# First attention stage of a two-layer transformer block: maxima rounded on GpSimd, merged products, 64-column masks, a split run of value matmuls, and another order on SyncE's queue

## The chip, the cores and the metric

One core of one Trainium2 chip. The metric is the device time of one execution in microseconds (us), the median of the runs shown. One execution was also taken by the hardware profiler; all rows below come from it.

The names of the profile: PE is TensorE's matmul stream and PEld its weight loads, DVE is VectorE, ACT is ScalarE, POOL is GpSimd, SP is SyncE, which here does nothing but issue DMAs.

## What is computed

Two pre-norm layers on x of 4 x 1024 tokens with 128 features. Only the first stage of the first layer is touched by the change, causal attention with 16 heads of 8 features and a bias that depends on the distance of query and key:

```python
q, k, v = (x @ W.T + b) split into 16 heads of 8
sim  = einsum('bhid,bhjd->bhij', q, k) + bias[i, j] * SCALE     # bias: 32 distance buckets
sim  = sim + causal                                             # -inf where j > i
out  = softmax(sim) @ v ;  out @ Wo.T + bo
```

Behind it come a routed feed-forward layer (16 leaves), a wide attention over its outputs, a second attention stage without a mask in this form, and a gated feed-forward layer. Those stages stay as they are.

## The kernel before

The stage is `attend_causal` (from line 508). It works through 64 heads (`NG`, 16 heads of 4 batches), one after the other, and in a pass of the loop, which this document calls head n's **pass**, the engines work on several heads at once. q and k are each split into three bf16 parts, so that a product of full precision is six bf16 products, stacked along the contraction: 48 rows (`PROWS`). Because 48 rows fit in half of the array, every operand is loaded twice, into partitions 0 to 47 and 64 to 111, and matmuls alternate between the two halves ("row groups"), which run side by side.

For each head:

- **Maxima** (lines 700 to 723). PE writes the masked scores of a query block against all keys into `psM` (two buffers of 1024 columns). There are five units, `MAXIMA = [(7,), (0, 6), (1, 5), (2, 4), (3,)]`, each of one or two query blocks. The mask is added by two further matmuls of 128 columns (`mask`, lines 694 to 698), whose operands lie in `masks`. DVE takes the row maxima with 8 reductions of 128 to 1024 columns (line 615), and then rounds minus the maximum to bf16 in two instructions, the value and the rest (lines 625 and 627). A unit waits until DVE has taken the unit two before it. The first unit of a head also waits for that head's loads (line 709).
- **Shift rows**. PE turns the rounded maxima with one small matmul (`rows`, line 733), ACT copies them to SBUF (line 666), and SP issues two small DMAs that put them under the head's q operand (`load_r`, line 505), where they act as two more contraction rows (50 in all).
- **Scores** (lines 736 to 752). Nine units of 512 columns into a ring of three banks (`psS`); a unit waits until ACT has taken the unit three before it. Those that touch the diagonal get the mask, again two matmuls of 128 columns. ACT takes the exponential (line 686) into `probs`. Unit 0 waits for the shift rows' DMA (line 739).
- **Bias near the diagonal**. POOL multiplies 8 blocks of `probs` (7 of 256 columns, one of 128) by the table of exponentiated biases (line 654). It also stages the values of the next head (line 645).
- **Values** (lines 754 to 776). 26 fp32 products in three parts, written to four column groups of the array (32 columns each), which run side by side; a product is two instructions for each of 10 wide (256 columns) and 16 narrow (128 columns) ones. Part 0 has 13 products, parts 1 and 2 six and seven. ACT copies the result (line 672), SP stores it (`store_o`, line 494).

The order on PE is written out by hand (lines 783 to 801): in head n's pass it does the scores of head n, the maxima of head n + 2 and the values of head n - 1:

```python
scores(n,0) scores(n,1) maxima(n+2,0) maxima(n+2,1) scores(n,2) scores(n,3)
values(n-1,0) rows(n+1) scores(n,4) maxima(n+2,2) scores(n,5) scores(n,6) maxima(n+2,3)
values(n-1,1) scores(n,7) scores(n,8) maxima(n+2,4) values(n-1,2)
```

SP's order is also by hand (lines 584 to 590). The loads of a head (`load_s`) are four DMAs of 96 KB; q and k have six buffers each (`BUFS`):

```python
for n in range(NG):
    load_s(n + 4)      # q and k of head n+4; waits for scores of head n-2
    store_o(n - 2)     # waits for ACT's copy of head n-2, in pass n
    load_r(n + 1)      # waits for ACT's copy of the shift rows, in pass n
```

So SP's round n ends in the middle of pass n, where `rows(n+1)` stands, and round n + 1 begins at once with the loads of head n + 5.

The opening stage `project_heads` builds the masks on POOL (lines 308 to 315, three selections), and SP swaps their halves with two DMAs (line 217).

## Time and profile before

| | us |
|---|---|
| median of 3 runs | 1780.42 (1780.28 to 1783.19) |
| profiled execution, its own time | 1783.86 |
| span of its trace, first to last instruction | 1782.1 |
| stage in question, from its first to its last matmul | 65.5 to 498.3 |
| share of the span: PE, DVE, ACT, POOL | 91%, 85%, 72%, 46% |
| granted TensorE clock, mean over the span | 0.943 |

The span is the time from the first to the last instruction; what lies between it and the execution's time (1.8 us) is outside the program. The share of an engine is the sum of its instructions' times, and those of overlapping matmuls are counted once, so that a PE at 91% may still have room in it. The granted clock is 1.00 at 2.4 GHz and 0.50 at 1.2 GHz. In the rows below, a line such as `L747 MATMUL heads_psS<-one_qS,one_kS 50*128 50x512 bf16 x2` is a group of instructions of line 747 that write tile `psS` from `qS` and `kS`, 50 rows of 128 stationary columns against 512 moving columns.

### The profile page before, as it was taken

The numbers are of one execution on the slowest core, as the hardware profiler recorded it, in microseconds if no ns is written. First come the engines' busy times: TensorE is split into PE (matmuls) and PEld (weight loads), VectorE is DVE, ScalarE is ACT, GpSimd is POOL, SyncE is SP. The second block draws the span as 40 slices with busy tenths as digits, with TensorE's granted clock in tenths as the row PEclk, the third lists the DMA queues.
The fourth block names the chain that finished last, engine by engine and source line by source line (L and its number), as shares of the span: only waits on it lengthen the run. The fifth ranks groups of instructions, "written<-read, shape, count | busy, mean of one in ns | idle before, by whom it ended". The sixth has DMA issues, their size and how long they took to land. (4 is left out here: it accounts for less than half of the span.)

```text
span 1782.1 us, 47495 instructions
## 1 busy us (share of the span) xinstructions
PE 1613.3 (91%) x18834; PEld 1038.2 (58%) x18858; DVE 1518.7 (85%) x2248; ACT 1276.2 (72%) x2523; POOL 817.8 (46%) x1533
## 2 busy tenths in 40 slices
PE   5599999999976999999899549999999999999966
PEld 3376667666665887877688314444444444444544
DVE  8699999999856999988677768999999999999735
ACT  6488878888834444454565628888989898998955
POOL 5488888888845001000340323444444444444446
PEclk9699999999965999999999868999999999999978
DMA  7522222323172766565000351111121121112031
GB/s 247 207 85 86 87 90 87 98 86 98 52 148 45 97 95 91 93 90 69 0 1 1 144 184 47 56 56 55 59 65 59 52 73 51 60 53 71 26 76 48
DMA packets 119910, 141.89 MB, mean 80 GB/s; under 512 B 22221, under 2 KB 80778, under 8 KB 119690
## 3 DMA queue, kind: packets, MB, share of 16 engines
q1 hardware_dynamic: 119258, 138.79, 30.8%
q8 instruction: 150, 2.46, 0.6%
q14 instruction: 70, 0.57, 0.1%
q10 hardware_dynamic: 432, 0.07, 0.0%
HBM read 92.70 MB, written 44.98 MB: 77 GB/s over the span
## 5 line engine op out<-in xcount | busy, mean ns | idle before, releaser
L888 DVE TENSOR_REDUCE heads_mx<-heads_psM 128x1 f32<-128x1024 f32 x512 | 602.1, 1219 | 48.4 <-PE heads_psM L979 32.2
L959 ACT ACTIVATE heads_probs<-heads_psS 128x512 f32<-128x512 f32 x1024 | 546.1, 601 | 77.7 <-PE heads_psS L1002 71.7
L928 POOL TENSOR_TENSOR heads_masked<-heads_probs,g_tri 128x128 f32<-128x128 f32 x512 | 233.7, 456 | 360.8 <-ACT heads_probs L959 360.7
L654 POOL TENSOR_TENSOR heads_probs<-heads_probs,one_ebias 128x256 f32<-128x256 f32 (+1 forms) x512 | 341.6, 689 | 76.8 <-ACT heads_probs L686 76.1
L615 DVE TENSOR_REDUCE heads_mx<-heads_psM 128x1 f32<-128x1024 f32 (+7 forms) x512 | 348.8, 748 | 23.7 <-PE heads_psM L697 23.0
L686 ACT ACTIVATE heads_probs<-heads_psS 128x512 f32<-128x512 f32 x576 | 316.3, 603 | 67.6 <-PE heads_psS L697 62.4
L979 PE MATMUL heads_psM<-three_kS,three_qS 48*128 48x512 bf16 x1024 | 230.4, 395 | 20.5 <-PEq L2050 11.6
L1002 PE MATMUL heads_psS<-three_qS,three_kS 50*128 50x512 bf16 x1024 | 238.0, 389 | 0.7 <-ACT heads_probs L959 0.3
L1510 ACT ACTIVATE trees_hid_hi<-trees_hid 128x512 fp32r<-128x512 f32 x192 | 121.6, 633 | 152.4 <-DVE trees_hid L1531 151.5
L1531 DVE SCALAR_TENSOR_TENSOR trees_hid<-trees_psH,g_b,trees_chosen 128x512 f32<-128x512 f32 x192 | 143.8, 749 | 31.8 <-DMA trees_chosen<-leaf_choice 15.1
L1027 PE MATMUL heads_psO<-heads_probs,heads_ones_only 128*32 128x128 f32 x1920 | 162.0, 284 | 0.0
L719 PE MATMUL heads_psM<-one_kS,one_qS 48*128 48x512 bf16 (+3 forms) x768 | 147.5, 334 | 14.8 <-PEq L2050 11.6
L1028 PE MATMUL heads_psO<-heads_probs,heads_v_ones 128*32 128x128 f32 x1920 | 155.9, 273 | 0.0
L769 PE MATMUL heads_psO<-heads_probs,heads_v_ones 128*32 128x256 f32 x1280 | 150.3, 394 | 2.2 <-POOL heads_probs L654 2.0
L747 PE MATMUL heads_psS<-one_qS,one_kS 50*128 50x512 bf16 (+3 forms) x768 | 141.1, 332 | 11.2 <-DMA one_qS<-heads_mrow 9.5
L1021 PE MATMUL heads_psO<-heads_probs,heads_ones_only 128*32 128x256 f32 x1280 | 148.7, 390 | 0.0
L1002 PEld LDWEIGHTS heads_psS<-three_qS,three_kS 50*128 50x128 bf16 x1024 | 69.5, 93 | 114.6 <-ACT heads_probs L959 55.3
L773 PE MATMUL heads_psO<-heads_probs,heads_v_ones 128*32 128x128 f32 x2048 | 136.1, 279 | 0.0
L1538 DVE SCALAR_TENSOR_TENSOR trees_hid_lo<-trees_hid,trees_hid_hi 128x512 fp32r<-128x512 f32 x192 | 134.0, 698 | 0.1
L1021 PE MATMUL heads_psO<-heads_probs,heads_v_ones 128*32 128x256 f32 x768 | 121.3, 394 | 0.0
L1027 PEld LDWEIGHTS heads_psO<-heads_probs,heads_ones_only 128*32 128x32 f32 x1920 | 72.6, 108 | 82.7 <-issue 82.7
L979 PEld LDWEIGHTS heads_psM<-three_kS,three_qS 48*128 48x128 bf16 x1024 | 56.4, 94 | 96.2 <-DVE heads_mx L888 64.5
(273 smaller groups left out, 3174.3 us busy)
## 6 DMA issues: line engine op xcount, KB each, us to landing
trees_chosen<-leaf_choice SPq DMA_DIRECT2D x96, 256.0 KB, 7.6
head_outputs<-g_small SPq DMA_DIRECT2D x128, 128.0 KB
one_qS<-q_parts SPq DMA_DIRECT2D x128, 96.0 KB
one_kS<-k_parts SPq DMA_DIRECT2D x128, 96.0 KB
three_qS<-q_parts SPq DMA_DIRECT2D x128, 96.0 KB
three_kS<-k_parts SPq DMA_DIRECT2D x128, 96.0 KB
q_parts<-g_w SPq DMA_DIRECT2D x8, 768.0 KB, 4.6
k_parts<-g_w SPq DMA_DIRECT2D x8, 768.0 KB, 5.8
```

What stands on the lines that cost most here:

```text
L615: last = dve.tensor_reduce(mx[:, p, qb:qb + 1], psM[(n * NM + i) % 2][:, at:at + w], AXX, ALU.max)
L654: pool.tensor_tensor(pr[:, a:a + w], pr[:, a:a + w], bass.AP(eb.tensor, eb.offset + NEAR - 1, [list(eb.ap[0]), [-1, w]]), ALU.mult).then_i ...
L686: act.activation(probs[n % 2][:, slot * CH:(slot + 1) * CH], ring.bank(i)[:, :], ACT.Exp).then_inc(slot_taken, 1)
L769: last = pe.matmul(out.rearrange("p (q w) -> p q w", w=P), v[:, kb, :], bass.AP(pr.tensor, a, [list(pr.ap[0]), [far - a, 2], [1, P]]), sta ...
L888: dve.tensor_reduce(mx[:, n % 2, k:k + 1], psM[k % 2][:, :], AXX, ALU.max, negate=True).then_inc(max_taken, 1)
L928: pool.tensor_tensor(masked[n % 2][:, kb, :], probs[n % 2][:, kb, kb * P:(kb + 1) * P], g["tri"][:, 0:P], ALU.mult).then_inc(near_done, 1)
L959: act.activation(probs[n % 2][:, kb, h * CH:(h + 1) * CH], ring.bank(i)[:, :], ACT.Exp).then_inc(slot_taken, 1)
L979: last = pe.matmul(psM[k % 2][:, h * CH:(h + 1) * CH], qS[u][r:r + PROWS, k * P:(k + 1) * P], kS[u][r:r + PROWS, h * CH:(h + 1) * CH], sta ...
L1002: pe.matmul(ring.bank(i)[:, :], kS[u][r:r + RROWS, kb * P:(kb + 1) * P], qS[u][r:r + RROWS, h * CH:(h + 1) * CH], start=True, stop=True).t ...
L1021: pe.matmul(out.rearrange("p (q w) -> p q w", w=P), v_ones[v][:, kb, :] if kb < c else ones_only[:, :], both, start=kb == 0, stop=False, t ...
L1027: pe.matmul(out[:, 0:P], ones_only[:, :], pr[:, c, :], start=False, stop=False, tile_position=(0, c * VW))
L1028: pe.matmul(out[:, P:2 * P], v_ones[v][:, kb, :], pr[:, b, :], start=False, stop=False, tile_position=(0, c * VW))
```

## The change

What it does, part by part:

1. **Rounding on POOL.** DVE's reductions give minus the maximum (`negate=True`). The two rounding instructions leave DVE; POOL does both (`minus_maxima`), for head n + 2 in pass n, between the last two of its bias products. For heads 0 and 1 it does them ahead of its loop.
2. **Merged products.** POOL's 8 bias products become 5 instructions: blocks 0 and 1 together, 7, 6, 2 and 3 together, 5 and 4 together (up to 512 columns).
3. **Masks of 64 columns.** A mask is still two matmuls with 128 stationary columns, but each covers 64 moving columns and not 128. Within a unit of the maxima the products of both row groups come first, in turn, and the masks at the end. The opening builds two tables with 14 small selections on POOL, each of which waits for the one before; SP copies with one DMA.
4. **Split value run.** Four parts of 6, 3, 10 and 7 products; part 1 stands right behind `rows`. Part 0 waits for four of the five bias products, part 2 for all.
5. **Maxima further ahead on PE.** The first two units are done for head n + 3, in the second half of pass n, and units 2, 3, 4 for head n + 2.
6. **Order on SP.** In each round the shift rows of head n + 1 come first, then the store of head n - 2, then the loads of head n + 4.

```diff
@@ SP's rounds
             for n in range(NG):
+                if n + 1 < NG:
+                    load_r(n + 1)
+                if n >= 2:
+                    store_o(n - 2)
                 if n + 4 < NG:
                     load_s(n + 4)
-                if n >= 2:
-                    store_o(n - 2)
-                if n + 1 < NG:
-                    load_r(n + 1)
@@ DVE
-                        last = dve.tensor_reduce(mx[...], psM[...][:, at:at + w], AXX, ALU.max)
+                        last = dve.tensor_reduce(mx[...], psM[...][:, at:at + w], AXX, ALU.max, negate=True)
...
-                dve.tensor_scalar(nm[:, p, 0, :], mx[:, p, :], -1.0, None, ALU.mult).then_inc(nm_hi, 1)
-                dve.wait_ge(nm_hi, n + 1)
-                dve.scalar_tensor_tensor(nm[:, p, 1, :], mx[:, p, :], -1.0, nm[:, p, 0, :], ALU.mult, ALU.subtract).then_inc(nm_ready, 1)
@@ POOL
+    NEARS = [((0, 1), 2), ((7,), 3), ((6,), 5), ((2, 3), 6), ((5, 4), 8)]
+            def minus_maxima(n):
+                p = n % 2
+                pool.wait_ge(max_taken, (n + 1) * NM)
...
+                pool.tensor_copy(nm[:, p, 0, :], mx[:, p, :]).then_inc(nm_hi, 1)
+                pool.wait_ge(nm_hi, n + 1)
+                pool.tensor_tensor(nm[:, p, 1, :], mx[:, p, :], nm[:, p, 0, :], ALU.subtract).then_inc(nm_ready, 1)
...
+                for blocks, unit in NEARS:
                     pool.wait_ge(slot_taken, ring.index(n, unit) + 1)
+                    weight(n, blocks)
+                    if unit == NEARS[-2][1] and n + 2 < NG:
+                        minus_maxima(n + 2)
@@ PE: masks, values
+                m2 = g["masks"][r:r + HALF, table, :]
+                for half in range(2):
+                    done = pe.matmul(out[:, half * HALF:(half + 1) * HALF], m2[:, half * P:(half + 1) * P], m2[:, 2 * P:2 * P + HALF],
+                                     start=False, stop=stop and half == 1)
...
-                    pe.wait_ge(near_done, (n + 1) * TPB)
+                    pe.wait_ge(near_done, n * len(NEARS) + NEAR_FIRST)
...
+                if part == 2:
+                    pe.wait_ge(near_done, (n + 1) * len(NEARS))
+    VALUES = [[(0, 0), (1, 0), (2, 0), (3, 0), (0, 1), (1, 1)], [(2, 1), (3, 1), (0, 2)],
+              [(1, 2), (2, 2), (3, 2), (0, 3), (1, 3), (2, 3), (3, 4), (0, 4), (1, 4), (0, 5)],
+              [(2, 4), (3, 3), (0, 6), (1, 5), (2, 5), (0, 7), (1, 6)]]
@@ PE's order
+            maxima(2, 0)
+            maxima(2, 1)
             for n in range(NG):
                 scores(n, 0)
                 scores(n, 1)
-                maxima(n + 2, 0)
-                maxima(n + 2, 1)
+                maxima(n + 2, 2)
+                maxima(n + 2, 3)
                 scores(n, 2)
                 scores(n, 3)
                 values(n - 1, 0)
                 rows(n + 1)
+                values(n - 1, 1)
                 scores(n, 4)
-                maxima(n + 2, 2)
+                maxima(n + 2, 4)
                 scores(n, 5)
                 scores(n, 6)
-                maxima(n + 2, 3)
-                values(n - 1, 1)
+                maxima(n + 3, 0)
+                values(n - 1, 2)
                 scores(n, 7)
                 scores(n, 8)
-                maxima(n + 2, 4)
-                values(n - 1, 2)
+                maxima(n + 3, 1)
+                values(n - 1, 3)
```

## Rows read from the trace of the kernel before

**Rows 1.** Busy time by stretch: the stage's settled part (engine busy us, granted clock, DMA share).

```profile
96.60:475.00 378.40, 368.56 (x6348) 261.05 (x6346) 363.68 (x583) 312.87 (x641) 319.55 (x525) 1.00 0.29 88
```

**Rows 2.** One line's instructions: ACT's copies of the shift rows, one for each head.

```profile
L666 ACT ACTIVATE heads_mrow<-heads_psS x64: 249/267/267, 72.6 to 484.2; 16x128 bf16<-16x128 f32 x64
```

**Rows 3.** Timeline of PE, one pass of a head (start us, us, instructions).

```profile
279.91 0.40 PE L747 MATMUL heads_psS<-one_qS,one_kS 50*128 50x512 bf16 x2
...
281.53 0.64 PE L769 MATMUL heads_psO<-heads_probs,heads_v_ones 128*32 128x256 f32 x8
...
282.64 0.22 PE L733 MATMUL heads_psS<-g_identb,heads_nm 128*16 128x128 bf16 x1
282.79 0.39 PE L747 MATMUL heads_psS<-one_qS,one_kS 50*128 50x512 bf16 x1
283.02 0.27 PE L697 MATMUL heads_psS<-g_masks 64*128 64x128 bf16 x2
283.13 0.39 PE L719 MATMUL heads_psM<-one_kS,one_qS 48*128 48x256 bf16 x2
...
284.27 0.30 PE L773 MATMUL heads_psO<-heads_probs,heads_v_ones 128*32 128x128 f32 x2
...
284.84 0.40 PE L747 MATMUL heads_psS<-one_qS,one_kS 50*128 50x128 bf16 x3
...
285.62 0.31 PE L773 MATMUL heads_psO<-heads_probs,heads_v_ones 128*32 128x128 f32 x3
...
286.19 0.40 PE L747 MATMUL heads_psS<-one_qS,one_kS 50*128 50x512 bf16 x2
```

**Rows 4.** Timeline of ACT in the same pass: the exponential of unit 0.

```profile
280.44 0.60 ACT L686 ACTIVATE heads_probs<-heads_psS 128x512 f32<-128x512 f32 x1 [0.26 <-PE heads_psS L697]
```

**Rows 5.** DVE: the reductions of one head (timeline), and the first rounding instruction (all 64).

```profile
281.35 5.42 DVE L615 TENSOR_REDUCE heads_mx<-heads_psM 128x1 f32<-128x1024 f32 x8
...
L625 DVE TENSOR_SCALAR heads_nm<-heads_mx x64: 171/704/710, 71.8 to 481.8; 128x8 bf16<-128x8 f32 x64
```

**Rows 6.** POOL: its products of 256 columns (96.6 to 475 us); the later stage's rounding.

```profile
L654 POOL TENSOR_TENSOR heads_probs<-heads_probs,one_ebias 128x256 f32<-128x256 f32 x409 | 287.8, 723 | 58.8 <-ACT heads_probs L686 58.4
...
L911 POOL TENSOR_TENSOR heads_nm<-heads_mx,heads_nm x64: 199/200/202, 1053.4 to 1685.9; 128x8 bf16<-128x8 f32 x64
```

**Rows 7.** Timeline of POOL in the opening stage (the wait stands in brackets).

```profile
16.80 1.27 POOL L327 TENSOR_TENSOR g_x<-g_x,g_bo 128x512 f32<-128x512 f32 x1 [7.52 <-DMA g_bo<-in_L_attn_bo]
```

**Rows 8.** Timeline of SP's queue, one round (start us, us of issuing).

```profile
283.19 1.38 SPq L505 DMA_DIRECT2D one_qS<-heads_mrow  x2
284.61 1.54 SPq L490 DMA_DIRECT2D one_qS<-q_parts  x2
286.20 1.41 SPq L490 DMA_DIRECT2D one_kS<-k_parts  x2
287.65 0.58 SPq L494 DMA_DIRECT2D head_outputs<-g_small  x1
```

**Rows 9.** SP's last load of head 5; DMA traffic from 83 to 91 us in 40 slices; one DMA's landing.

```profile
84.61 1.41 SPq L490 DMA_DIRECT2D one_kS<-k_parts  x2
...
GB/s 0 0 0 21 0 0 0 31 72 41 82 164 123 82 72 133 164 123 102 164 123 51 113 133 133 41 20 0 0 0 0 0 0 9 12 0 82 21 0 0
...
g_x<-in_L_attn_x SPq DMA_DIRECT2D x8, 256.0 KB, 3.9
```

**Rows 10.** Waits, 96.6 to 475 us (total us, times, longest): scores for the shift rows' DMA.

```profile
PEld heads_psS L747 <- DMA one_qS<-heads_mrow: 17.3, 30, 1.7
```

**Rows 11.** PE around the one fall of the clock in the stage (timeline; busy time by stretch).

```profile
234.12 0.40 PE L747 MATMUL heads_psS<-one_qS,one_kS 50*128 50x512 bf16 x2 [1.44 <-DMA one_qS<-heads_mrow]
...
235.30:238.70 3.40, 3.40 (x35) 2.06 (x34) 2.11 (x3) 1.86 (x5) 1.86 (x3) 0.50 0.22 69
...
241.96 0.40 PE L747 MATMUL heads_psS<-one_qS,one_kS 50*128 50x512 bf16 x2
```

**Rows 12.** Timeline of PE at the stage's start: the shift rows of head 1.

```profile
80.21 0.28 PE L733 MATMUL heads_psS<-g_identb,heads_nm 128*16 128x128 bf16 x1
```

More of the change, by code:

```diff
@@ L60 @@
 SHIFTS = 2
+MASKW = 2 * P + HALF
 EARLY = 2
@@ L693, in _, with mask @@
         def _(pe):
-            def mask(out, r, table):
-                for s in range(2):
-                    done = pe.matmul(out, g["masks"][r:r + HALF, s, 0, :], g["masks"][r:r + HALF, s, table, :], start=False, stop=s == 1)
+            def mask(out, r, table, stop=True):
+                m2 = g["masks"][r:r + HALF, table, :]
+                for half in range(2):
+                    done = pe.matmul(out[:, half * HALF:(half + 1) * HALF], m2[:, half * P:(half + 1) * P], m2[:, 2 * P:2 * P + HALF],
+                                     start=False, stop=stop and half == 1)
                 return done
@@ L710, in maxima @@
                 ps = psM[k % 2]
-                at = 0
+                runs, ends, at = ([], []), [], 0
                 for qb in MAXIMA[i]:
@@ L715, in maxima @@
                         a, z = max(at, bank * CH), min(at + w, (bank + 1) * CH)
-                        if a >= z:
-                            continue
-                        r, ends = HALF * bank, z == at + w
-                        last = pe.matmul(ps[:, a:z], qS[u][r:r + PROWS, qb * P:(qb + 1) * P], kS[u][r:r + PROWS, a - at:z - at], start=True, stop=not ends)
-                        if ends:
-                            last = mask(ps[:, z - P:z], r, 1)
-                    at += w
+                        if a < z:
+                            runs[bank].append((qb, a, z, a - at))
+                    at += w
+                    ends.append(at)
+                for j in range(max(len(of) for of in runs)):
+                    for bank in range(2):
+                        if j < len(runs[bank]):
+                            qb, a, z, first = runs[bank][j]
+                            r = HALF * bank
+                            pe.matmul(ps[:, a:z], qS[u][r:r + PROWS, qb * P:(qb + 1) * P], kS[u][r:r + PROWS, first:first + z - a],
+                                      start=j == 0, stop=j + 1 == len(runs[bank]) and (bank + 1) * CH not in [-(-e // CH) * CH for e in ends])
+                for half in range(2):
+                    for z in ends:
+                        r, at = HALF * ((z - 1) // CH), z - P + half * HALF
+                        m2, later = g["masks"][r:r + HALF, 0, :], [e for e in ends if z < e <= -(-z // CH) * CH]
+                        last = pe.matmul(ps[:, at:at + HALF], m2[:, half * P:(half + 1) * P], m2[:, 2 * P:2 * P + HALF], start=False,
+                                         stop=half == 1 and not later)
                 last.then_inc(maxima_done, 1)
@@ L749, in scores @@
                     if diagonal:
-                        last = mask(ps[:, at:at + P], r, 2)
+                        last = mask(ps[:, at:at + P], r, 1)
                     at += count
@@ L804, in _ @@
             values(NG - 1, 2)
+            values(NG - 1, 3)
 def attend_full(nc, m, g, hand, gather):
```

72 lines of the change are left out of this document (44 added, 28 removed).

## The prediction

> **What bounds the kernel now.** I read the busy time by stretch first. In the settled part of the stage PE and DVE are both nearly always busy, ACT and POOL are not [rows 1]. Two engines at the limit need a closer look, so next comes the length of a pass: the copies of the shift rows give 411.6 us for 63 passes, 6.53 us each [rows 2], while the pass in PE's timeline takes 6.28 (279.91 to 286.19) [rows 3]. The difference, 0.25 us a pass or some 15 us, is stalls, and the list of waits names one: scores that wait for the shift rows' DMA, 17.3 us in 30 times [rows 10].
>
> Who sets 6.28? DVE's 8 reductions take 5.42 [rows 5]. The first rounding instruction takes 0.704 in the middle and 0.171 at best [rows 5], so some 0.53 us of it is a wait inside the instruction. (The Trainium skill, "SBUF — State Buffer", section "Who interferes with whom", says that such an instruction and one of GpSimd exclude each other from a shared port pair; by that rule the wait ends with a product on POOL, and the trace agrees in size, 0.72 for a product.) DVE's own work is therefore about 5.42 + 0.17 + 0.17 = 5.76, and it has slack. PE has none: its pass is a chain of stretches [rows 3]. From scores 0 to the values 1.62, values part 0 1.11, rows 0.15, the second row stretch 1.48, part 1 0.57, the third row stretch 0.78, part 2 0.57: 6.28. The first of these hangs on ACT as well: the exponential of unit 0 begins at 280.44 and lasts 0.60 [rows 4], and only then may unit 3 use its bank.
>
> **The change, part by part**, for a pass in which nothing is late.
>
> *DVE* drops to 5.42. As PE sets the pass, that gives nothing by itself. *POOL* is busy 319.55 us in 378.4, 5.5 a head [rows 1]; the merged products handle as many columns, so at worst they cost the same, at best three fixed parts less; the rounding adds 2 x 0.20 [rows 6]. That is 5.9 at most, below the pass that follows; POOL is covered by PE, with little to spare. If it were not, part 2 of the values would wait for the last product.
>
> *Masks.* Two masks of 128 columns lie 0.11 us apart from start to next start (283.02 to 283.13) [rows 3]. No matmul of 64 columns is in the trace. Bounds: nothing saved (the weights still have 128 columns), or half, 0.055 a pair. I take half, since the 512 columns at 282.79 hold the next start off by 0.23, four times the 0.055 of one mask [rows 3]: the time goes with columns. The rule against it is in the Trainium skill, "TensorE: Matmul & The Clock Gate", section "LDWEIGHTS": loading takes about P / 1.2 ns for P stationary columns, an estimate of 107 ns for 128. By that rule no mask would get shorter, and those of today would lie further apart than the trace has them.
>
> *PE's stretches.* First: two pairs on the chain through ACT, 1.62 - 0.11 = 1.51. Values: one narrow instruction takes about 0.11 of its column group. Part 0 has 8 such turns in the fullest group and not 10, so 1.11 - 0.22 = 0.89 to the rows. Parts 0 and 1 with the rows between them have 8 in each group, so if the rows' matmul (16 columns) leaves the other groups running, they take 1.22 to the next scores; if all drain, 0.89 + 0.15 + 0.57 = 1.61. I take 1.22: rows follow the values today at a normal distance. Part 2 has 6 turns, not 4: 0.57 + 0.22 = 0.79. Part 3: 0.57. Second row stretch: only one of five units has its work moved off, and the fuller row group then holds three units with masks and 512 columns: 3 x 0.28 + 0.21 + 0.09 = 1.14. Third: 0.78 - 0.11 = 0.67. Sum 1.51 + 1.22 + 1.14 + 0.79 + 0.67 + 0.57 = 5.90, against 6.28. The split of the values gives back part of what the masks and the even row groups win.
>
> *SP, the step that I think decides.* Today the loads of head n + 4 are issued right behind the shift rows of head n, in the middle of pass n - 1, and are needed at the start of pass n + 2: over two passes. Afterwards they come behind the shift rows of head n + 1, in the middle of pass n, one whole pass later; and PE wants them earlier, since maxima unit 0 of head n + 4 now stands in the second row stretch of pass n + 1. That is from both sides a loss, and the wait is ahead of everything on PE's queue: values part 2, units 7 and 8, all of the next pass.
>
> How long is the way from the rows' matmul to the landed loads? Matmul to SP's first issue 0.55 (282.64 to 283.19) [rows 3, 8]. The two row DMAs with the gap 1.42, the store now ahead of the loads 0.58 + 0.07, four loads 3.00 (284.61 to 287.61) [rows 8]. Landing after the last issue: nowhere does an engine wait for these loads, so I bound it. Head 5's last load is issued until 86.02, and traffic goes on until about 88.4: at least 2.4. Above: 3.9, what a DMA of 256 KB takes from its issue [rows 9]. I take 3.2, the middle. With 0.04 to wake PE: 0.55 + 1.42 + 0.65 + 3.00 + 3.2 + 0.04 = 8.86.
>
> And from that maxima unit to the next rows' matmul, on PE: the unit and the change of mode 0.37, part 2 0.79, third stretch 0.67, part 3 0.57, first stretch 1.51, part 0 0.89: 4.80. The unit in pass n + 1 waits for loads behind the rows of pass n, and these rows come 4.80 after the unit of pass n - 1. So two passes take 8.86 + 4.80 = 13.66, one takes **6.83**, not 5.90, and PE stands still for 0.93 us in each.
>
> *The shift rows* have then more time: today they are issued 3.0 us ahead of scores 0 (283.19 to 286.19) [rows 3, 8], afterwards about 3.9. Most of their 15 us go; they are inside the 6.83.
>
> *Start and end.* Rows of head 1 stand at 80.21 [rows 12]. Two more units of maxima ahead of the loop cost DVE about 1.2 each, so 82.6. The first late unit is that of pass 1: 82.6 + 8.9 = 91.5. 59 passes later, at 91.5 + 59 x 6.83 = 494.5, comes the last one that waits; two more rows follow at + 4.8 + 5.9 = 505.2, against 484.2 today [rows 2]. The stage ends **21 us** later.
>
> *Opening.* Fourteen selections, each behind the one before, cost POOL perhaps 7 us; it waits 7.52 us there today for a DMA [rows 7], so nothing; without that cover a few us. One DMA fewer on SP lies off the path too.
>
> *Clock.* A stall of 1.44 us was followed by a stretch at 0.50 (1.2 GHz), and the next pass took 241.96 - 234.12 = 7.84, or 1.56 more than 6.28 [rows 11]; it is the only one in the settled stage. With a stall near 1 us in each pass, and passes that drift into long and short ones (only the sum of two is fixed), I allow one fall in 20 heads or so: 4 us.
>
> **Sum.** 21 + 4 = 25 us on the profiled execution's own time, 1783.86 (its span is 1782.1, 1.8 less): 1809. That execution lies 3.4 above the median of the runs, so the median becomes 1780.4 + 25 = **1805**.
>
> **Rivals.**
>
> A. *The loads are in time* and nothing else is late: the pass is 5.90 plus the 0.25 of stalls that remain for the shift rows. From 82.6, 62 passes of 6.15 end at 463.9, against 484.2: 20 us less, 1760. It speaks for it that PE, DVE and POOL all get room. Against it: the way would have to shrink from 8.86 to 2 x 5.90 - 4.80 = 7.0, and without any landing it is already 5.66, so landing would have to take 1.3 us, where traffic alone goes on for 2.4 [rows 9]. Should I have misread which head is loaded in which round, this is what is left. 13 in 100.
>
> B. *The clock.* The stall in each pass lets the clock fall in every second head: 30 x 1.56 = 47 in place of 4, some 1848. For: the one fall [rows 11]. Against: thirty waits, and one fall [rows 10, 11]. 8 in 100.
>
> C. *No change.* A pass of 6.53 as now, if the way is 8.26, with a landing of 2.6, the low bound nearly. The point from which the sign turns is there. 7 in 100.
>
> D. *The masks don't shrink*, as the rule above would have it: 0.11 more in the first stretch, 0.11 in the third, 0.06 in the unit itself: 4.80 becomes 5.08, the pass 6.97, and 59 x 0.14 = 8 us are added: 1813. 15 in 100 of the chance, inside the forecast's side.
>
> E. *The change does nothing*, because PE would wait elsewhere by the same amount: only by chance; it is within C.
>
> **How the numbers follow.** The forecast as summed has 57 in 100, D 15, B 8, C 7, A 13. The bounds of the landing, 2.4 and 3.9, move a pass by -0.40 and +0.35, so -24 and +21 us: 1781 to 1826; with D and a part of B above. The range is 1776 to 1848; it leaves out A and the worst of B. A measurement of this kernel tells 0.2%, 3.6 us, from no change. Faster by more: 0.14 (A and a little of C). Same: 0.07. Slower: 0.79.
>
> **What would show it.** In the changed kernel's list of waits, PE or its weight loads wait for the loads of q or k (the matmuls of the maxima, released by "DMA one_qS<-q_parts" or "one_kS<-k_parts"), in about 60 places of 0.9 us in the mean; the wait for the shift rows' DMA is nearly gone. The copies of the shift rows lie 6.8 apart. DVE shows idle time of about 1.4 us a head that ends with PE's maxima. SP's timeline has rows, store, loads in this order, and the loads' last issue ends some 5 us behind the first row DMA. Passes of 5.9 with no such wait would prove A; a granted clock of 0.50 in many stretches of the stage would prove B. A mask pair 0.055 us apart from the next matmul proves the halving, 0.11 proves D. If the rows' matmul is followed by part 1 only after a gap of 0.1 us or more, the value groups drained, and 0.4 us are to be added to each pass's natural length, but not to the 13.66.

## The result, and the profile after

The changed kernel takes 1831.91 us (median of 4 runs, 1821.83 to 1836.86) where the kernel before, run beside it, takes 1780.35. The ratio is 1.0278, with a 95% interval of 1.0254 to 1.0303: 51.5 us slower, where 25 were forecast. The profiled execution took 1830.29, with a span of 1828.4 and a mean granted clock of 0.932.

The busy time of the same stretch as in [rows 1] comes first (us busy and instructions of PE, weight loads, DVE, ACT, POOL, then granted clock, DMA share, GB/s):

```profile
96.60:475.00 378.40, 317.89 (x5662) 213.98 (x5662) 290.41 (x415) 265.11 (x571) 280.60 (x416) 0.94 0.25 78
```

PE was busy 368.56 us of the 378.40 before and is 317.89 now; DVE fell from 363.68 to 290.41, and the clock from 1.00 to 0.94. No engine has too much work: all of them wait. How long the stage has become stands in ACT's copies of the shift rows, the line that answers to [rows 2] (durations in ns, first and last start in us):

```profile
L701 ACT ACTIVATE heads_mrow<-heads_psS x64: 248/249/267, 72.3 to 533.4; 16x128 bf16<-16x128 f32 x64
```

From 72.3 to 533.4 it is 461.1 us, against 411.6: 49.5 more. The spans differ by 46.3, so the whole loss lies in this stage, and 3 us come back elsewhere. (The medians differ by 51.5, since the profiled execution of the kernel before lies 3.5 above its median and that of the changed kernel 1.6 below.) The list of waits from 90 to 510 us names the place (us in total, times, longest):

```profile
ACT heads_probs L721 <- PE heads_psS L733: 124.7, 166, 5.4
POOL heads_probs L680 <- ACT heads_probs L721: 99.9, 97, 4.6
DVE heads_mx L637 <- PE heads_psM L768: 91.7, 88, 3.9
PE heads_psM L762 <- DMA one_kS<-k_parts: 58.4, 31, 3.6
...
PEld heads_psS L794 <- DMA one_qS<-heads_mrow: 1.4, 7, 0.2
```

ACT, POOL and DVE wait for PE, and PE for one thing, the loads of k ahead of a maxima unit: 31 times, 1.9 us in the mean. The wait for the shift rows' DMA, 17.3 us in [rows 10], is down to 1.4. Read from behind, the chain is POOL on ACT, ACT on PE, PE on the DMA; only the last of these says what to change.

SP's queue over two rounds shows how it comes about (start, us of issuing):

```profile
443.13 1.40 SPq L527 DMA_DIRECT2D one_qS<-heads_mrow  x2
444.57 0.58 SPq L516 DMA_DIRECT2D head_outputs<-g_small  x1
445.20 1.53 SPq L512 DMA_DIRECT2D one_qS<-q_parts  x2
446.76 1.41 SPq L512 DMA_DIRECT2D one_kS<-k_parts  x2
450.98 1.40 SPq L527 DMA_DIRECT2D one_qS<-heads_mrow  x2
```

and PE's timeline of the same stretch:

```profile
445.61 0.39 PE L762 MATMUL heads_psM<-one_kS,one_qS 48*128 48x512 bf16 x2 [1.83 <-DMA one_kS<-k_parts]
...
450.25 0.22 PE L780 MATMUL heads_psS<-g_identb,heads_nm 128*16 128x128 bf16 x1
```

The order is rows, store, loads, as in the diff; the last load is issued 5.0 us behind the first row DMA. The wait in brackets ends with a load of the round before. From that unit to the next rows' matmul PE needs 450.25 - 445.61 = 4.64. Passes alternate: 5.75 to 5.9 us, then 7.8 to 8.1, where nothing else comes in between. Only from 126 to 160 us are they nearly even, five passes of 6.5 to 7.0 with stalls of 0.6 to 1.0, and no fall of the clock comes there.

The second loss is the clock. One of the stalls and what follows it (PE's timeline, then busy time by stretch):

```profile
190.63 0.39 PE L762 MATMUL heads_psM<-one_kS,one_qS 48*128 48x512 bf16 x2 [2.06 <-DMA one_kS<-k_parts]
```

```profile
192.30:195.70 3.40, 3.40 (x46) 2.31 (x41) 2.12 (x5) 2.39 (x5) 1.45 (x2) 0.50 0.34 116
195.70:199.00 3.30, 3.30 (x65) 2.20 (x63) 3.09 (x5) 2.88 (x7) 2.19 (x3) 1.00 0.03 8
```

PE stood for 2.06 us, and 1.7 us later the granted clock is 0.50 (1.2 GHz) for 3.4 us: PE is busy throughout, but 46 matmuls go through where 65 do at 1.00. The kernel before has one such fall in the settled stage [rows 11], the changed one has 12, two of them 6.8 us long.

### The profile page after: what moved, and what is told of

Its sections match the earlier page's. It is cut to its first block and busy times, and to the rows that moved or that the text cites. A ratio compares the mean times of both kernels' runs of the same rounds, so it can differ in the third digit from the quotient of the medians.

```text
span 1828.4 us, 47344 instructions
## 1 busy us (share of the span) xinstructions
PE 1600.4 (88%) x18858; PEld 1014.3 (55%) x18858; DVE 1475.2 (81%) x2120; ACT 1260.1 (69%) x2523; POOL 815.4 (45%) x1480
## 5 line engine op out<-in xcount | busy, mean ns | idle before, releaser
L637 DVE TENSOR_REDUCE heads_mx<-heads_psM 128x1 f32<-128x1024 f32 (+7 forms) x512 | 357.9, 753 | 116.2 <-PE heads_psM L768 108.0
L680 POOL TENSOR_TENSOR heads_probs<-heads_probs,one_ebias 128x512 f32<-128x512 f32 (+2 forms) x320 | 313.9, 998 | 114.9 <-ACT heads_probs L721 107.4
L762 PE MATMUL heads_psM<-one_kS,one_qS 48*128 48x512 bf16 (+3 forms) x768 | 139.4, 353 | 84.8 <-DMA one_kS<-k_parts 60.2
L818 PE MATMUL heads_psO<-heads_probs,heads_v_ones 128*32 128x256 f32 x1280 | 157.6, 400 | 1.1 <-POOL heads_probs L680 1.1
L1081 PE MATMUL heads_psO<-heads_probs,heads_v_ones 128*32 128x128 f32 x1920 | 155.9, 273 | 0.0
L822 PE MATMUL heads_psO<-heads_probs,heads_v_ones 128*32 128x128 f32 x2048 | 148.4, 295 | 0.1
L794 PE MATMUL heads_psS<-one_qS,one_kS 50*128 50x512 bf16 (+3 forms) x768 | 145.6, 346 | 1.4 <-ACT heads_probs L721 1.0
L1074 PE MATMUL heads_psO<-heads_probs,heads_v_ones 128*32 128x256 f32 x768 | 121.3, 395 | 0.0
L1080 PEld LDWEIGHTS heads_psO<-heads_probs,heads_ones_only 128*32 128x32 f32 x1920 | 72.6, 108 | 82.3 <-issue 82.3
```

The costliest lines, as they stand in the source:

```text
L637: last = dve.tensor_reduce(mx[:, p, qb:qb + 1], psM[(n * NM + i) % 2][:, at:at + w], AXX, ALU.max, negate=True)
L680: pool.tensor_tensor(at, at, by, ALU.mult).then_inc(near_done, 1)
L818: last = pe.matmul(out.rearrange("p (q w) -> p q w", w=P), v[:, kb, :], bass.AP(pr.tensor, a, [list(pr.ap[0]), [far - a, 2], [1, P]]), sta ...
L1074: pe.matmul(out.rearrange("p (q w) -> p q w", w=P), v_ones[v][:, kb, :] if kb < c else ones_only[:, :], both, start=kb == 0, stop=False, t ...
L1080: pe.matmul(out[:, 0:P], ones_only[:, :], pr[:, c, :], start=False, stop=False, tile_position=(0, c * VW))
L1081: pe.matmul(out[:, P:2 * P], v_ones[v][:, kb, :], pr[:, b, :], start=False, stop=False, tile_position=(0, c * VW))
```

## Experiments

All are compared with the kernel before; its medians beside them were 1782.28 (first four), 1782.37 (next four) and 1783.3 (last three). "Stage" is the time from the first to the last copy of the shift rows, in the profile of each; "pass" is the usual distance of two passes in which nothing is late.

| kernel | us | ratio [95%] | stage | pass |
|---|---|---|---|---|
| before | 1780.4 | 1 | 411.6 | 6.28 |
| the change | 1831.9 | 1.0278 [1.0254, 1.0303] | 461.1 | 5.75 / 8.0 |
| loads first | 1775.1 | 0.9946 [0.9927, 0.9964] | 403.9 | 5.75 |
| before + new queue order | 1781.6 | 0.9993 [0.9978, 1.0008] | 408.8 | 6.28 |
| the change, filled | 1810.5 | 1.0155 [1.0137, 1.0174] | 446.5 | 6.65 / 7.1 |
| the change, store last | 1797.2 | 1.0074 [1.0048, 1.01] | 432.6 | 5.75 / 7.4 |
| one head sooner | 1760.8 | 0.9881 [0.9867, 0.9896] | 388.2 | 5.78 |
| + rounding on DVE | 1788.6 | 1.0036 [1.0022, 1.005] | 418.5 | 6.49 |
| + masks twice | 1811.4 | 1.0161 [1.0146, 1.0176] | 444.5 | 6.85 |
| + values in three parts | 1801.1 | 1.0116 [1.0095, 1.0136] | 428.0 | 6.58 |
| + masks of 128 columns | 1773.7 | 0.9940 [0.9919, 0.9961] | 404.3 | 6.15 |
| + head outputs sooner | 1749.8 | 0.9811 [0.9795, 0.9826] | 381.3 | 5.78 |
| before + order + one sooner | 1784.4 | 1.0012 [0.9998, 1.0025] | 410.0 | 6.28 |

**Is it the queue?** The first kernel undoes nothing but SP's order.

```diff
             for n in range(NG):
-                if n + 1 < NG:
-                    load_r(n + 1)
-                if n >= 2:
-                    store_o(n - 2)
                 if n + 4 < NG:
                     load_s(n + 4)
+                if n >= 2:
+                    store_o(n - 2)
+                if n + 1 < NG:
+                    load_r(n + 1)
```

> The changed kernel with one thing undone: SyncE's round is again loads of head n + 4, store, shift rows. Theory (the late head loads are the whole loss): no wait of PE for q or k is left, a pass takes the 5.8 us that the short passes of the changed kernel show, plus about 0.25 for late shift rows; the stage gets (7.26 - 6.05) x 59 = 71 us shorter than in the changed kernel, the time is about 1760, and the clock doesn't fall more than once or twice in the stage. Rival (the PE order, the split values or the work on GpSimd cost the time): the time stays above 1800.

1775.09 us, 56.8 below the changed kernel: the order costs more than the whole loss, and the rest of the change is a small gain. It is smaller than expected. Many passes are 5.75, but they average 6.34, and the waits from 90 to 500 us say why:

```profile
PEld heads_psS L794 <- DMA one_qS<-heads_mrow: 37.4, 49, 2.3
```

The shift rows are late now, 49 times. In this order they are issued behind the loads; where their two DMAs of 4 KB landed after 1.15 us at best, many took 1.5 to 2.5, and two 3.5. (All landings here are counted from the end of the last issue.) A shorter pass has made the second-latest thing the latest.

The same order in the kernel before:

```diff
+                if n + 1 < NG:
+                    load_r(n + 1)
+                if n >= 2:
+                    store_o(n - 2)
                 if n + 4 < NG:
                     load_s(n + 4)
-                if n >= 2:
-                    store_o(n - 2)
-                if n + 1 < NG:
-                    load_r(n + 1)
```

> The kernel before with SyncE's new order and nothing else of the change. Theory (the order costs only together with the maxima unit of head n + 3 in pass n): loads of head n + 4 land some 11.3 us behind the start of pass n and are needed at the start of pass n + 2, 12.6 us behind it, so PE doesn't wait for them except when they land late; the time is 1775 to 1790. Rival (the order alone is the loss): some 1830.

1781.57, no change. So it is not the order by itself: it takes the order together with something else of the change. That the something is the maxima unit that now wants its head a pass earlier is read from the trace, where PE's wait stands at that unit and nowhere else; no run undoes PE's order alone. It agrees with the prediction's "from both sides a loss".

**Is the stall all, or does the clock add to it?** The changed kernel, with useless matmuls ahead of the wait (they write to a bank that the unit itself then overwrites):

```diff
                 if i == 0:
+                    if 3 <= n:
+                        v = (n - 3) % BUFS
+                        for _ in range(4):
+                            for r, a in ((0, 0), (HALF, CH)):
+                                pe.matmul(psM[k % 2][:, a:a + CH], qS[v][r:r + PROWS, 0:P],
+                                          kS[v][r:r + PROWS, 0:CH], start=True, stop=True)
                     pe.wait_ge(s_loaded[u], (n // BUFS + 1) * 64)
```

> The changed kernel with 8 matmuls of 512 columns (two row groups, about 0.9 us) of no use ahead of PE's wait for a head's loads, written where the unit's own products go afterwards. Theory (two passes together are fixed at 13.8 us by the way through SyncE, they drift into one of 5.8 and one of 8.0, and the long stall lets the clock fall): the short pass becomes 6.65, the long one 7.15 and more even, the idle time is filled, the clock hardly falls in the stage; the mean pass is 6.9 and the time about 1831 - 59 x 0.36 = 1810, so more work makes it faster. Rival (PE's work is what counts): 0.9 x 61 = 55 us slower, 1885.

1810.52: 21.4 us faster by doing more. The busy time of its stage:

```profile
98.00:525.00 427.00, 405.91 (x7163) 271.82 (x7160) 338.80 (x482) 315.72 (x681) 333.69 (x490) 1.00 0.26 81
```

The clock is 1.00 throughout, not one fall, and the stage is 14.6 us shorter, although each head carries eight matmuls more. The loop through SyncE is as long as before: the 26 pairs of passes without a load of 512 KB (more on these below) took 13.85 us each, those of the changed kernel without a fall 13.83. So what went is the falls, and the gain is a lower bound on what the clock cost in the changed kernel.

The way itself, made shorter by the store (0.58 and a gap):

```diff
                 if n + 1 < NG:
                     load_r(n + 1)
-                if n >= 2:
-                    store_o(n - 2)
                 if n + 4 < NG:
                     load_s(n + 4)
+                if n >= 2:
+                    store_o(n - 2)
```

> The changed kernel with the round shift rows, loads, store: the loads no longer stand behind the store, so the way through SyncE is 0.65 us shorter. Theory: two passes together take 13.8 - 0.65 = 13.15, one 6.6, stalls get shorter and the clock falls less often; 20 to 35 us less than the changed kernel, 1797 to 1812. Rival (the landing of the loads doesn't follow the time of issue, since the queue is limited by something else): within 5 us of 1831.

1797.19, at the fast end of what was expected, and 34.7 us below the changed kernel. The wait for k is 35.9 us in 34 times (90 to 490 us, since the stage is shorter) and not 58.4 in 31, and the clock falls 4 times in the stage, not 12. Moving 0.65 us out of a way that closes every second pass is worth 0.33 a pass, 19 us in 59. The rest is 15; eight falls less, at the 1.6 worked out below, would be 13 of it.

**Both late things at once.** The new order as it is, but each round loads one head further ahead; there are six buffers, so there is room.

```diff
-            for n in range(EARLY, 4):
+            for n in range(EARLY, 5):
                 load_s(n)
...
-                if n + 4 < NG:
-                    load_s(n + 4)
+                if n + 5 < NG:
+                    load_s(n + 5)
```

> The changed kernel as it is, its queue order too (shift rows, store, loads), but each round of SP loads head n + 5 and not n + 4, and the opening loads one head more. Theory: both of the late things are gone, the loads because they have a whole pass more, the shift rows because nothing is issued ahead of them. With the loads in time but ahead of the shift rows, 60 passes took 6.33 each, and the undisturbed ones among them 5.75 (scores of head 2 at 94.9, of head 61 at 468.2). All of them at 5.75 to 5.80 would put head 61 at 94.9 + 59 x 5.8 = 437, 31 us sooner: 1742 to 1748, no wait of PE for a DMA in the stage and no fall of the clock in it. Rival: the passes over 5.75 came from something other than the place of the shift rows in the queue (ACT, POOL or the traffic of the loads itself): then some 1775, as with the loads first. A second rival: the loads, now ahead of their time, hold up the landing of the shift rows by traffic, since both are then in flight together more often: 1755 to 1770.

1760.76: 71 us below the changed kernel, and 1.2% faster than the kernel before, though not the 1742 to 1748 of the first theory. The time lies in the second rival's range. The usual pass is 5.78 as expected, but the mean is 6.07. No wait for q or k is left in the list from 100 to 430 us. Of the 17 us that the 59 passes take beyond 5.78, 12.6 are in three places, one of which stands in SP's queue so:

```profile
217.09 1.41 SPq L512 DMA_DIRECT2D one_kS<-k_parts  x2
218.54 0.58 SPq L1171 DMA_DIRECT2D g_qkT<-head_outputs  x1
219.21 1.38 SPq L527 DMA_DIRECT2D one_qS<-heads_mrow  x2
```

Right ahead of the shift rows goes a transfer of 512 KB, the outputs of a batch's 16 heads; the rows landed after 4.4 us, the two passes from there took 8.75 and 8.34, and the clock fell in them (the other places: 8.59 and 8.15, with a fall, and 7.69, without; all from scores to scores). That is a cause none of my theories had. Only the 4.5 us that are left, in passes of 5.8 to 6.5, may be the second rival's traffic of the loads.

From here on, three parts of the change (the rounding, the width of the masks, the split of the values) are undone one at a time in this kernel. The merged products and PE's order stay in all of them, so their worth was not measured.

**Rounding on DVE.**

```diff
+                dve.wait_ge(max_taken, (n + 1) * NM)
+                dve.wait_ge(block_taken, (n + 1) * (TPB - NM))
+                if n >= 2:
+                    dve.wait_ge(slot_done, ring.rows(n - 2) + 1)
+                dve.tensor_scalar(nm[:, p, 0, :], mx[:, p, :], 1.0, None, ALU.mult).then_inc(nm_hi, 1)
+                dve.wait_ge(nm_hi, n + 1)
+                dve.scalar_tensor_tensor(nm[:, p, 1, :], mx[:, p, :], 1.0, nm[:, p, 0, :], ALU.mult, ALU.subtract).then_inc(nm_ready, 1)
...
-            minus_maxima(0)
-            minus_maxima(1)
...
-                    if unit == NEARS[-2][1] and n + 2 < NG:
-                        minus_maxima(n + 2)
```

> The kernel with head n + 5 loaded each round, and in it the rounding of the maxima back on DVE, one part of the change undone alone. DVE's reductions take 5.42 a pass, the pass 5.75. The two roundings bring 2 x 0.17 at best, 5.76, and 0.17 + 0.70 with the wait inside the first one, 6.29. Theory (DVE becomes the bound with them, the port wait included): passes of 5.9 to 6.3, so 8 to 30 us more than with the rounding on POOL, 1752 to 1775. Rival (the prediction's view, that this part gives nothing as PE sets the pass): within 4 us of it.

1788.58, 27.8 more, inside the 8 to 30 of the theory, though the pass of 6.49 is longer than its 6.3. DVE's timeline shows a pass without a gap:

```profile
150.52 5.62 DVE L637 TENSOR_REDUCE heads_mx<-heads_psM 128x1 f32<-128x1024 f32 x8
156.18 0.17 DVE L646 TENSOR_SCALAR heads_nm<-heads_mx 128x8 bf16<-128x8 f32 x1
156.38 0.70 DVE L648 SCALAR_TENSOR_TENSOR heads_nm<-heads_mx,heads_nm 128x8 bf16<-128x8 f32 x1
```

5.62 + 0.17 + 0.70 is 6.49, the pass. The wait has moved to the second instruction, the one with two inputs, whose shortest in the kernel before is 0.166. In all 50 heads between 100 and 430 us it ends 0.02 us behind a product on POOL; in the kernel before it is the first instruction that does so, in all 51, 0.03 us behind. (By the Trainium skill, "SBUF — State Buffer", section "Who interferes with whom", a DVE instruction with two inputs in SBUF contends with a GpSimd instruction that reads there; this trace agrees, with 0.70 against 0.17.)

**Masks, first the wrong way round: each 64-column mask twice.**

```diff
                 for half in range(2):
+                    pe.matmul(out[:, half * HALF:(half + 1) * HALF], m2[:, half * P:(half + 1) * P], m2[:, 2 * P:2 * P + HALF],
+                              start=False, stop=False)
                     done = pe.matmul(out[:, half * HALF:(half + 1) * HALF], m2[:, half * P:(half + 1) * P], m2[:, 2 * P:2 * P + HALF],
```

> The kernel with head n + 5 loaded each round, with each 64-column mask matmul issued twice (the second adds the same mask again, so the output is not the reference's), which gives back about the 0.055 us per pair that the narrower masks saved. The prediction's stretches hold some 5 pairs on PE's path of a pass (two in the first, two in the third, one in the unit of maxima): 5 x 0.03 to 5 x 0.055 = 0.15 to 0.28 a pass if PE sets the pass, 9 to 17 us in all. Rival: PE has slack in the pass of 5.75 beside DVE's 5.42 and ACT, and less than 5 us are added.

1811.37, 50.6 more, three times the most that was expected. PE's timeline has the masks 0.03 us apart:

```profile
117.68 0.19 PE L733 MATMUL heads_psS<-g_masks 64*128 64x64 bf16 x1
117.71 0.19 PE L735 MATMUL heads_psS<-g_masks 64*128 64x64 bf16 x1
117.74 0.19 PE L733 MATMUL heads_psS<-g_masks 64*128 64x64 bf16 x1
117.77 0.19 PE L735 MATMUL heads_psS<-g_masks 64*128 64x64 bf16 x1
```

and the pass is 1.07 longer, which is 32 more masks at 33 ns: every added one counts in full. I then took this for the worth of the narrow masks. It isn't: issuing an operation twice is not the opposite of making it half as wide. So the width alone was undone, with zeros beside the 64 columns:

```diff
-MASKW = 2 * P + HALF
+MASKW = 2 * P + 3 * HALF
...
-                    done = pe.matmul(out[:, half * HALF:(half + 1) * HALF], m2[:, half * P:(half + 1) * P], m2[:, 2 * P:2 * P + HALF],
+                    done = pe.matmul(out, m2[:, half * P:(half + 1) * P], m2[:, 2 * P + HALF - half * HALF:3 * P + HALF - half * HALF],
```

(the same in the maxima; the table's triangle stands 64 columns further right).

> The kernel that loads head n + 5 each round, with the masks 128 columns wide again: the moving side gets 64 columns of zeros before or behind its 64, so the same values are added by as many instructions, in the same order, and only the width is undone. Doubling the 32 masks of 64 columns took 1.07 us more a pass, 33 ns each. Theory: the price of a mask goes with its columns, 55 to 60 ns at 128 and 33 at 64, so 32 x 0.022 to 0.027 = 0.7 to 0.85 a pass at most, and 0.5 at least, since the kernel before needed 6.28 where 5.75 is needed now: 30 to 50 us more, 1790 to 1811. Rival (the prediction's sum: only some 5 pairs lie on PE's path, 0.3 a pass): 15 to 20 us more, 1776 to 1781. Second rival (the rule that only the stationary columns count): nothing.

1773.70: 12.9 more, and a pass of 6.15, 0.38 more. The theory drawn from the doubled masks is wrong. The rival, which is the prediction's own sum, is near: its 0.3 a pass is 0.38, and the time is 2 us below its 1776 to 1781. The pair is 0.06 apart:

```profile
157.70 0.22 PE L733 MATMUL heads_psS<-g_masks 64*128 64x128 bf16 x1
157.76 0.21 PE L733 MATMUL heads_psS<-g_masks 64*128 64x128 bf16 x1
```

59 passes of 0.38 are 22 us; the stage grew by 16. At least a part of the difference is that the shift rows are late less often in a longer pass (their wait, from 100 to 430 us, is 5.0 us instead of 20.7).

**Values in three parts.**

```diff
-    NEAR_FIRST = 4
-    VALUES = [[(0, 0), (1, 0), (2, 0), (3, 0), (0, 1), (1, 1)], [(2, 1), (3, 1), (0, 2)],
...
+    NEAR_FIRST = 5
+    VALUES = [[(0, 0), (1, 0), (2, 0), (3, 0), (0, 1), (1, 1), (2, 1), (3, 1), (0, 2), (1, 2), (2, 3), (3, 4), (0, 3)],
...
                 rows(n + 1)
-                values(n - 1, 1)
```

> The kernel with head n + 5 loaded each round, with the values in the three parts of the kernel before. By the prediction's working parts 0 and 1 with the rows take 1.22 and part 2 0.79, part 3 0.57, together 2.58; before it was 1.11 + 0.15 + 0.57 + 0.57 = 2.40. By that the split costs 0.18 a pass, and this kernel is up to 10 us faster than with the split. Against it: the rows come 0.4 later behind a longer part 0, and the shift rows have less time. Rival: the split is worth something (rows sooner, no bubble between the row groups), and this kernel is 5 to 20 us slower.

1801.09: 40.3 more, the wrong way round from my sum and twice the rival's most. PE's and POOL's timelines show the reason, the first of them with 0.73 us of standing:

```profile
115.79 0.64 PE L818 MATMUL heads_psO<-heads_probs,heads_v_ones 128*32 128x256 f32 x8 [0.73 <-issue]
```

```profile
114.27 0.20 POOL L671 TENSOR_TENSOR heads_nm<-heads_mx,heads_nm 128x8 bf16<-128x8 f32 x1
114.42 1.26 POOL L680 TENSOR_TENSOR heads_probs<-heads_probs,one_ebias 128x512 f32<-128x512 f32 x1
```

Part 0 of the old division has blocks that only the fifth product weights. Merged, that product takes 1.26 us and stands behind the rounding; it ends at 115.68, and PE's values begin at 115.79. The profile puts the wait down to "issue", but PE resumes with POOL's end, and the same stall comes 47 times between 100 and 430 us (0.73 in the median). The new division lets part 0 go after four products. It makes merging and rounding on POOL affordable; which of these two needs it more no run tells, since both were in place.

**The 512 KB.** Issued right behind that round's shift rows:

```diff
                 if n + 1 < NG:
                     load_r(n + 1)
+                if n > HEADS and n % HEADS == 6:
+                    gather.load_num(sp, n // HEADS - 1)
                 if n >= 2:
                     store_o(n - 2)
                 if n + 5 < NG:
                     load_s(n + 5)
...
-                if n > HEADS and n % HEADS == 6:
-                    gather.load_num(sp, n // HEADS - 1)
```

> The kernel that loads head n + 5 each round, and the 512 KB of head outputs that three rounds of the stage load (heads 22, 38, 54) are issued right behind the shift rows of that round and no longer behind the loads. In that kernel two passes behind each such load took 8.75 and 8.34 us where the others take 5.78: the shift rows landed 4.4 us after their issue and not 1.15, and the clock fell with the stall. Theory: the transfer (4.9 us) is over before the next shift rows are issued 5.78 later, the loads of q and k that follow it have a pass to spare, and up to 3 x 5.5 = 16 us go: 1744 to 1752. Rival: the transfer and the loads behind it together are still under way when the next shift rows come (the round moves 900 KB), and the delay stays: 1758 to 1762.

1749.75, a further 11.0 us and inside the theory's range, the best of all: 1.9% below the kernel before, where the change itself is 2.8% above it. The stage, from the end of the opening's slow clock to the next fall:

```profile
91.40:466.90 375.50, 355.55 (x6803) 245.27 (x6799) 336.38 (x484) 318.96 (x688) 336.90 (x497) 1.00 0.31 95
```

Not all of it went: the pass of head 24 is still 7.68, its shift rows landed after 3.3 us, behind the end of the 512 KB and the loads of that round; the three collisions still hold some 5 us.

**The queue alone**, in the kernel before:

```diff
-            for n in range(EARLY, 4):
+            for n in range(EARLY, 5):
...
+                if n + 1 < NG:
+                    load_r(n + 1)
+                if n >= 2:
+                    store_o(n - 2)
+                if n + 5 < NG:
+                    load_s(n + 5)
-                if n + 4 < NG:
-                    load_s(n + 4)
...
```

> The kernel before, with only SP's order of the change (shift rows, store, loads) and head n + 5 loaded each round. It tells how much of the gain of that kernel over the kernel before comes from the queue alone. The kernel before stands still for the shift rows some 15 us (30 waits, 17.3), its pass is 6.28 without them and 6.50 with. Theory: the queue alone is worth at most 12 us, 1768 to 1773, and the other parts of the change the 8 to 12 below that. Rival: the late shift rows of the kernel before have another cause than what is issued ahead of them: 1778 to 1782.

1784.37, no gain, and above the ranges of both theory and rival. Its passes are 6.28 almost without exception, so the small waits of [rows 10] are gone; but the three passes at the 512 KB take 9.7, 8.4 and 9.4 where the kernel before has 9.2, 7.5 and 7.6, and the first pass 10.1 for 8.7. So the queue without the rest gives nothing, the rest without it 0.5%, both together 1.2%. The kernel before with the 512 KB moved was not run, so how much of the last 11 us needs the change is open.

## Why the prediction was right and where it was wrong

**The mechanism** is the one forecast: loads behind the shift rows, one head late for a maxima unit moved ahead. Rival A is refuted. Its condition, loads in time, holds in "one head sooner", which took 1760.8; A had said 1760 too, but that is luck: it had passes of 6.15 throughout, where most are 5.78 and the rest of the time is in the three collisions and the opening.

**The way of 8.86** was 9.0 in the median and 9.10 in the mean, over 57 heads: rows to SP's first issue 0.73 (0.55 in the sum, which is right for the kernel before throughout; in the changed one ACT's copy starts 0.45 behind the rows' matmul and not 0.26), row DMAs 1.40 (1.42), to the loads 0.67 (0.65), the loads 2.98 (3.00), landing 3.34 (3.2). The bounds of 2.4 and 3.9 were wide, and their middle was good.

**From unit to rows** 4.64 was measured, 4.80 forecast. Two passes: 9.10 + 4.64 = 13.74, forecast 13.66. Taken in pairs from the rows of head 4 to those of head 62, seventeen pairs of passes without a fall took 235.2 us, 13.83 each.

**The natural pass of 5.90** is 5.78. The sum had one term too long, parts 0 and 1 with the rows. By "one head sooner", first stretch 1.55 (1.51), parts 0 and 1 with the rows 1.05 (1.22), second stretch 1.15 (1.14), part 2 0.80 (0.79), third 0.67 (0.67), part 3 0.57 (0.57). PE's timeline there, from one rows' matmul to the next:

```profile
107.70 0.22 PE L780 MATMUL heads_psS<-g_identb,heads_nm 128*16 128x128 bf16 x1
...
108.07 0.39 PE L794 MATMUL heads_psS<-one_qS,one_kS 50*128 50x512 bf16 x1
...
109.22 0.30 PE L822 MATMUL heads_psO<-heads_probs,heads_v_ones 128*32 128x128 f32 x1
...
110.02 0.40 PE L794 MATMUL heads_psS<-one_qS,one_kS 50*128 50x128 bf16 x3
...
110.69 0.30 PE L822 MATMUL heads_psO<-heads_probs,heads_v_ones 128*32 128x128 f32 x1
...
111.26 0.40 PE L794 MATMUL heads_psS<-one_qS,one_kS 50*128 50x512 bf16 x2
...
112.81 0.64 PE L818 MATMUL heads_psO<-heads_probs,heads_v_ones 128*32 128x256 f32 x8
...
113.49 0.22 PE L780 MATMUL heads_psS<-g_identb,heads_nm 128*16 128x128 bf16 x1
```

The value groups don't drain around the rows' matmul. The masks' halving is right too: 0.033 us for one of 64 columns, 0.06 for one of 128, and 0.38 a pass, where rival D put 0.28 of the sum down to it. Rival D is refuted: both kinds of mask load 128 stationary columns, and only the moving columns differ. (The Trainium skill, "TensorE: Matmul & The Clock Gate", section "LDWEIGHTS", gives the length of a load, an estimate of 107 ns for 128 columns. The traces agree with that length, 94 to 100 ns in the mean for a load of the masks. What fails is the prediction's reading that masks must then lie so far apart: with the masks doubled, four of them start 0.03 us apart, each with its own load.)

**The step that failed** is the clock's: "I allow one fall in 20 heads or so: 4 us". There were 12 falls in 59 passes, and the passes that hold them took 23.8 us too many, where 4 were allowed. The forecast put the last rows, without the clock, at 505.2 (21 us later than before); they came at 533.0, 27.8 later. The 12 pairs of passes that hold a fall took 187.7 us, where 12 x 13.66 is 163.9: 23.8 more. The 17 others account for 3.0; some 1 us is left, for the opening and the one pass ahead of the pairs. Three of the 12 pairs also hold a load of 512 KB and have 9.1 of the 23.8, a part of which is the load's and not the clock's. The other nine lost 1.6 each in the mean (1.5 in the eight with a fall of 3.4 us, 2.9 in the one with 6.8), the price that [rows 11] gave (1.56). So the price of one fall was right, and their number was wrong, by four times. Rival B, every second head, had 2.5 times too many. (Of the 27 us between 1805 and 1831.9, some 5 are the difference between profiled execution and median told above.)

Why was the number wrong? I took "thirty waits, and one fall" [rows 10, 11] as evidence against B. But those thirty were 0.6 us in the mean, and the one that was followed by a fall was the longest of them: 1.71 at the weight load, as [rows 10] counts, and 1.44 at the matmul, as [rows 11] has it. The three longest (1.71, 1.49, 1.45) are those behind the three loads of 512 KB, and one of the three was followed by a fall; one in three of some thirty long stalls would have been ten falls. The prediction itself had said that only the sum of two passes is fixed; it then worked with a stall of 0.93 in each. A pair in which one pass is natural puts its whole stall, 13.7 - 2 x 5.78 = 2.1 us, in one place, and the rows to compare with are those longest waits, not the mean. The filled kernel shows it the other way: same queue, same late loads, no fall. Why a given stall of about 2 us is followed by a fall and the next is not, stays open.

**DVE and POOL** were judged too lightly, without harm to the number, since the loads covered both. The prediction had DVE with slack, so that moving its rounding "gives nothing by itself": in a pass of 5.78 it gives 28 us, and in [rows 5] the sum with the wait inside, 5.42 + 0.70 + 0.17 = 6.29, was already the pass of 6.28. A wait inside an instruction is not slack if POOL will be busy next time too. It also said that the split of the values "gives back part": the split is worth 40 us, because it keeps POOL's last product off PE's path. I had costed POOL by its busy time (5.9 at most) and not by when its fourth and fifth products end.

**Opening and end.** Rows of head 1 stood at 82.27 (82.6 forecast), and the loads of head 4 had landed at 90.83 (91.5). What I had not seen is that the opening's stretch of slow clock would be longer: 37.5 us (59.1 to 96.6) against 27.3 (57.8 to 85.1), and 34.1 in most of the variants. The two units moved ahead of the loop may be the reason, but no run shows it by itself, and the two kernels with SP's order changed and PE's not have 30.7. Scores of head 2 came at 96.7, in "one head sooner" at 93.9, in the kernel before at 91.5; so the change costs some 2.4 us there even with all loads in time. The opening's fourteen selections took 5.3 us (7 forecast) and cost nothing that shows: POOL's wait behind them fell from 7.52 to 2.16, and the first copy of the shift rows is at 72.3, before at 72.6.

## What to carry to other kernels

When a change moves a request back in a queue and its user forward, add both and write the loop that they close; here it gave the mean pass without a fall to 1.2% (6.83, measured 6.91). If that loop spans two iterations, the stall gathers in one of them, so price its consequences (the clock above all) for twice the mean. And once one wait is removed, look at what lands second-latest before moving anything else: the change was worth 1.9% with loads one head sooner and the 512 KB moved, and minus 2.8% without. (The 512 KB's share of the 1.9% may not need the change.)

## What the runs showed of the hardware that I had not expected

A kernel with eight more matmuls of 512 columns per head ran 21 us faster, since PE's clock stayed at 1.00 (2.4 GHz) over the same late loads. Two DMAs of 4 KB landed 1.15 us behind their last issue at best, and 4.4 us behind it where one of 512 KB stood right ahead of them on the same queue (that one takes 4.7 to 5.0 us from its issue in the best kernel). A DVE instruction of 8 columns took 0.70 us instead of 0.17 where a product on POOL had just begun, and ended with that product, whichever of the two rounding instructions it was. Weight loads of 0.09 to 0.10 us started 0.03 us apart, and so did their matmuls of 64 columns.
